# Both FFN layers of a macaron block in steps of two blocks or row tiles, on one core

## What is computed

```python
x = x + 0.5 * ffn(layernorm(x), Wr, bias, Wg, Wu, Wd, sWg, sWu, sWd)
x = x + attention(layernorm(x), ...)        # 16 heads of width 16, causal, with a decay
x = x + 0.5 * ffn(layernorm(x), ...)        # the same weights once more

def ffn(x):                                 # 1024 rows, 16 experts, hidden width 128
    probs = softmax(x @ Wr.T + bias)
    w, idx = top_k(probs, 2);  w = w / (sum(w) + 1e-9)
    y[t, e] = (silu(x[t] @ Wg[e]) * (x[t] @ Wu[e])) @ Wd[e]
    routed[t] = sum over the two chosen e of w * y[t, e]
    return routed + silu(x @ sWg) * (x @ sWu) @ sWd      # one shared expert for all rows
```

## Time and profile before

| | |
|---|---|
| median of 3 ordinary runs | 350.92 us (347.88 to 352.57) |
| profiled execution, from first to last instruction | 375.8 us |
| TensorE, matmul | 276.6 us busy, 74% |
| VectorE | 244.9 us, 65% |
| ScalarE | 167.1 us, 44% |
| GpSimd | 130.5 us, 35% |
| mean granted TensorE clock | 0.878 of full |

### The profile page before, as it was taken

One profiled execution on the slowest core, in us unless ns is written; L12 is line 12 of the kernel. 1 busy time (PEld: TensorE's weight loads), 2 busy tenths in 40 slices (PEclk: granted clock), 3 DMA queues, 4 the chain that ended last, 5 costly groups with the idle time before them and its releaser, 6 DMA issues.

```text
span 375.8 us, 6430 instructions
## 1 busy us (share of the span) xinstructions
PE 276.6 (74%) x1911; PEld 199.4 (53%) x1911; DVE 244.9 (65%) x800; ACT 167.1 (44%) x433; POOL 130.5 (35%) x181
## 2 busy tenths in 40 slices
PE   1747649888882587989999999987384598898710
PEld 1537428877771254555444444654273287787700
DVE  8686865757666871658888885466841266667616
ACT  3566604434443155357666666662321044444300
POOL 7027841555456003300445200000077125555630
PEclk9966757999997799898999999999696599999965
DMA  7996654434400617980534400000022603344127
GB/s 249 385 388 191 261 161 161 120 99 130 131 19 15 210 42 185 197 250 26 113 88 85 86 3 1 2 3 0 0 101 98 195 15 110 108 138 131 31 81 254
DMA packets 29861, 45.69 MB, mean 122 GB/s; under 512 B 5323, under 2 KB 22961, under 8 KB 29444
## 3 DMA queue, kind: packets, MB, share of 16 engines
q1 hardware_dynamic: 24164, 33.41, 29.2%
q0 software_dynamic: 5664, 11.87, 10.9%
HBM read 27.98 MB, written 20.61 MB: 129 GB/s over the span
## 4 chain that ended last, share of the span: by engine, by line
PE 54%; DVE 19%; issue 7%; DMA 7%; ACT 7%; POOL 2%; another core or an unknown queue 2%; SPq 1%; POOLq 0%; DVEq 0%; ACTq 0%
PE bank L313 23%; PE bank L1015 5%; PE bank L1054 5%; PE bank L1028 4%; PE bank L320 4%; PE bank L947 4%; PE bank L871 3%; DVE wl L1212 3%; DMA yg<-results 2%; DVE res L1384 2%; PE bank L1032 2%; DMA stk_q<-parts_d 1%; DVE xn L1227 1%; PE bank L856 1%
## 5 line engine op out<-in xcount | busy, mean ns | idle before, releaser
L568 POOL DMA_INDIRECT results<-ysb,xp x62 | 61.5, 993 | 75.4 <-DVE ysb L1351 55.6
L1440 DVE CUSTOM_DVE_ANT_0 bank<-bank,dec 128x512 f32<-128x512 f32 (+3 forms) x128 | 59.8, 518 | 18.2 <-PE bank L1015 18.0
L1312 DVE TENSOR_TENSOR hm<-sg,bank 128x128 f32<-128x128 f32 x78 | 22.3, 286 | 51.4 <-ACT sg L654 30.7
L820 ACT ACTIVATE ct<-bank 128x512 f32<-128x512 f32 (+1 forms) x96 | 45.0, 520 | 22.0 <-PE bank L1032 21.9
L654 ACT ACTIVATE sg<-bank 128x128 f32<-128x128 f32 x78 | 21.5, 276 | 63.8 <-PE bank L313 54.4
L557 POOL DMA_INDIRECT slots_x<-xn,slot x32 | 34.1, 1064 | 33.3 <-DVE slot L1289 24.3
L313 PE MATMUL bank<-wh,xT_h 128*128 x124 | 41.3, 333 | 3.7 <-DVE xT_l L1339 2.9
L700 ACT ACTIVATE xT_h<-bank 128x256 fp32r<-128x256 f32 x62 | 23.8, 386 | 34.7 <-PE bank L947 30.6
L871 PE MATMUL bank<-ident,hm 128*128 128x128 f32 x78 | 23.7, 304 | 20.4 <-issue 11.3
L1015 PE MATMUL bank<-stk_q,stk_k 96*128 96x512 bf16 (+3 forms) x128 | 34.9, 310 | 2.1 <-DMA stk_q<-parts_d 1.8
L313 PE MATMUL bank<-wh,hT_h 128*128 (+1 forms) x78 | 30.7, 394 | 7.2 <-issue 2.7
(11 more groups left out here) (186 smaller groups left out, 681.5 us busy)
## 6 DMA issues: line engine op xcount, KB each, us to landing
xp<-slots_x SPq DMA_DIRECT2D x30, 257.0 KB
w_raw<-in_experts SPq DMA_DIRECT2D x17, 384.0 KB, 8.4
yg<-results SPq DMA_DIRECT2D x16, 256.0 KB, 4.8
slots_x<-zeros SPq DMA_DIRECT2D x2, 1285.0 KB, 11.8
parts_d<-part SPq DMA_DIRECT2D x6, 384.0 KB, 3.2
stk_k<-parts_d SPq DMA_DIRECT2D x8, 192.0 KB, 3.8
stk_q<-parts_d POOLq DMA_DIRECT2D x8, 192.0 KB, 4.9
slots_x<-zeros SPq DMA_DIRECT2D x1, 1413.5 KB, 7.8
```

What stands on the lines that cost most here:

```text
L568: pool.indirect_dma_start(results, where, ysb[c % RING][:], None, bounds_check=4 * N - 1, oob_is_err=False).then_inc(s_ys[c % RING], 16)
L820: act.activation(ct[n % 6][:, a:b], bank[2 + i][:, 0:b - a], ACT.Exp).then_inc(s_exp, 1)
L1440: dve.tensor_tensor_reduce(s_i, s_i, dec[:, SEQ - w:SEQ], 1.0, NEG, ALU.add, ALU.max, mmax[g % 2][:, n % G * QT + i:n % G * QT + i + 1])\
```

## The change

Every step of the two FFN loops takes two blocks (or two row tiles) in place of one:

- The shared expert's loop has 4 steps, the block loop has NQ = 16 steps (the last one holds a single block) plus 3 for the pipeline. The order within a step stays the same: transposes of pair q, gate and up of q - 1, hidden transposes of q - 2, down products of q - 3.
- A stage's result of a pair fills one bank: 512 words for `xT`, gate and up, and down, 256 for the hidden transpose. The matmuls are the same in number and size.
- ScalarE and VectorE take both blocks in one instruction: `xT` high and low and `ysb` are 512 wide, Silu, `hm`, `hT` high and low 256, the addition to `res` 512.
- The semaphores count pairs. GpSimd waits once a pair and then issues two scatters, one for each block.
- XRING goes from 12 to 16 blocks (8 pairs loaded ahead), RING from 4 to 6. The registers with the expert addresses are still loaded four at a time.
- In the first layer the splits of weights are spread differently over the steps: two high splits on ScalarE and three low splits on VectorE per pair step.
- Some buffers share memory in another way, to make room. Nothing else changes.

```diff
-    RING = 4
-    XRING = 12
+    RING = 6
+    XRING = 16
+    REGS = 4
...
-        def over_blocks(step):
-            for b in range(NB + 3):
-                step(b, [0 <= b - k < NB for k in range(4)])
+        def blocks_in(q):
+            return min(2, NB - 2 * q)
+        def halves(tile, n):
+            return tile[:, 0:n * D].rearrange("p (i k t) -> p i k t", i=n, k=2)
+        def over_pairs(step):
+            for q in range(NQ + 3):
+                step(q, [0 <= q - k < NQ for k in range(4)])
...                                                             SyncE
-                    last = 2 * (q - QRING) + 1
-                    sp.wait_ge(s_xt, f * NB + last + 1)
-                    for b in (last - 1, last):
+                    old = q - QRING
+                    sp.wait_ge(s_xt, f * NQ + old + 1)
+                    for b in (2 * old, 2 * old + 1):
                         sp.wait_ge(*scattered(f, b))
                     load(q)
...                                                             GpSimd
                         pool.wait_ge(*landed(f, c))
-                        pool.wait_ge(s_ye, f * NB + c + 1)
-                        where = bass.IndirectOffsetOnAxis(ap=xb[c % XRING][:, D:XW].bitcast(U32), axis=0)
-                        pool.indirect_dma_start(results, where, ysb[c % RING][:], None, ...)
+                        pool.wait_ge(s_ye, f * NQ + c + 1)
+                        for i in range(blocks_in(c)):
+                            b = 2 * c + i
+                            where = bass.IndirectOffsetOnAxis(ap=xb[b % XRING][:, D:XW].bitcast(U32), axis=0)
+                            pool.indirect_dma_start(results, where, ysb[c % (RING // 2)][:, i, :], None, ...)
...                                                             ScalarE
-                act.activation(sg[par][:], bank[2 + par][:, 0:F], ACT.Silu).then_inc(s_sg, 1)
+                act.activation(sg[j % 2][:, 0:n, :], halves(bank[2 + j % 2], n)[:, :, 0, :], ACT.Silu).then_inc(s_sg, 1)
-                for i in range(NT + 2):
+                for i in range(NP_ + 1):
...
-                    if f == 0 and EARLY + i <= E:
-                        split_high(EARLY + i)
+                    if f == 0:
+                        for q in (EARLY + 2 * i, EARLY + 2 * i + 1):
+                            if q <= E:
+                                split_high(q)
...                                                             TensorE
-                three(pe, bank[2 + par][:, 0:GU], xs, ws, None).then_inc(s_gu, 1)
+                for i in range(n):
+                    mm = three(pe, bank[2 + j % 2][:, i * GU:(i + 1) * GU], xs(i), ws(i), None)
+                mm.then_inc(s_gu, 1)
-                pe.transpose(bank[4 + par][:, 0:P], hm[par][:], ident[:]).then_inc(s_ht, 1)
+                for i in range(n):
+                    mm = pe.transpose(bank[4 + j % 2][:, i * P:(i + 1) * P], hm[j % 2][:, i, :], ident[:])
+                mm.then_inc(s_ht, 1)
-                        for k in range(KT):
-                            mm = pe.transpose(bank[b % 2][:, k * P:(k + 1) * P],
-                                              xb[b % XRING][:, k * P:(k + 1) * P], ident[:])
+                        for i in range(blocks_in(q)):
+                            for k in range(KT):
+                                mm = pe.transpose(bank[q % 2][:, (i * KT + k) * P:(i * KT + k + 1) * P],
+                                                  xp[q % QRING][:, i, k * P:(k + 1) * P], ident[:])
...                                                             VectorE
-                dve.tensor_tensor(hm[par][:], sg[par][:], bank[2 + par][:, F:GU], ALU.mult).then_inc(s_hm, 1)
+                dve.tensor_tensor(hm[j % 2][:, 0:n, :], sg[j % 2][:, 0:n, :], halves(bank[2 + j % 2], n)[:, :, 1, :],
+                                  ALU.mult).then_inc(s_hm, 1)
...
-                        for q in (i + 1,) if i < 6 else (2 * i - 5, 2 * i - 4):
+                        for q in range(3 * i + 1, min(3 * i + 4, E + 1)):
                             split_low(q)
...
-                        dve.tensor_copy(ysb[r][:], bank[6 + (j - 3) % 2][:, 0:D]).then_inc(s_ye, 1)
+                        dve.tensor_copy(ysb[c % (RING // 2)][:, 0:n, :],
+                                        bank[6 + (j - 3) % 2][:, 0:n * D].rearrange("p (i d) -> p i d", i=n))\
+                            .then_inc(s_ye, 1)
```

More of the change, by code:

```diff
@@ L141, in macaron_kernel @@
         r0.close()
[L142 to L155, removed]
+        xp = [sb(f"xp{i}", [P, 2, XW], F32, r2) for i in range(4)]
+        xT = [[sb(f"xT{j}_{i}", [P, 2, KT, P], F32R, r2) for i in "hl"] for j in range(2)]
+        hT = [[sb(f"hT{j}_{i}", [P, 2, P], F32R, r2) for i in "hl"] for j in range(2)]
+        r0 = ExitStack()
+        lgT = sb("lgT", [E, N], F32, r0)
+        r0.close()
+        sg = [sb(f"sg{i}", [P, 2, F], F32, r2) for i in range(2)]
+        hm = [sb(f"hm{i}", [P, 2, F], F32, r2) for i in range(2)]
+        r0 = ExitStack()
+        lg = sb("lg", [P, NT, E], F32, r0)
+        pr = sb("pr", [P, NT, E], F32, r0)
+        tmp = sb("tmp", [P, NT, E], F32, r0)
+        oh = sb("oh", [P, 2, NT, E], F32, r0)
+        ohs = sb("ohs", [P, NT, E], BF16, r0)
+        big = sb("big", [P, NB * E], F32, r0)
+        r0.close()
+        ysb = [sb(f"ysb{i}", [P, 2, D], F32, r2) for i in range(RING // 2)]
+        iota_i = sb("iota_i", [P, NB + 1], I32, r2)
         mx = sb("mx", [P, NT], F32, r2)
@@ L197, in macaron_kernel @@
         r5.close()
-        xp += [sb(f"xp{i}", [P, 2, XW]) for i in range(2, QRING)]
+        xp += [sb(f"xp{i}", [P, 2, XW]) for i in range(4, QRING)]
         xb = [xp[i // 2][:, i % 2, :] for i in range(XRING)]
@@ L913, in w_s @@
                     return (wh, wl)[b][:, E, k * GU:(k + 1) * GU]
-                for i in range(NT + 2):
+                for i in range(NP_ + 2):
                     j = f * NJ + i
-                    if i < NT:
-                        gate_up(j, j % 2, f == 0 and i < 2, rows(i), w_s)
-                    if 0 <= i - 1 < NT:
-                        hidden_turn(j - 1, (j - 1) % 2, f == 0 and i - 1 < 2)
-                    if 0 <= i - 2 < NT:
+                    if i < NP_:
+                        gate_up(j, lambda h: rows(2 * i + h), lambda h: w_s)
+                    if 0 <= i - 1 < NP_:
+                        hidden_turn(j - 1)
+                    if 0 <= i - 2 < NP_:
                         if i - 2 >= 2:
-                            pe.wait_ge(s_ysh, f * NT + i - 3)
-                        down(j - 2, j % 2, lambda b: (wh, wl)[b][:, E, KT * GU:WE])
-                pe.wait_ge(s_ysh, (f + 1) * NT)
+                            pe.wait_ge(s_ysh, f * NP_ + i - 3)
+                        down(j - 2, lambda h, b: (wh, wl)[b][:, E, KT * GU:WE])
+                pe.wait_ge(s_ysh, (f + 1) * NP_)
                 if f == 0:
@@ L933, in ffn, with step @@
                 keep_busy(bank[5], 6)
-                def step(b, live):
-                    j, n = f * NJ + NT + b, f * NB + b
-                    if b % RING == 0 and b < NB:
-                        regs = [pe.alloc_register(f"expert{f}_{i}") for i in range(b, min(b + RING, NB))]
+                def step(q, live):
+                    j = f * NJ + NP_ + q
+                    b = 2 * q
+                    if b % REGS == 0 and b < NB:
+                        regs = [pe.alloc_register(f"expert{f}_{i}") for i in range(b, min(b + REGS, NB))]
                         pe.load(regs, bexi[0:1, b:b + len(regs)])
@@ L1328, in ffn @@
                         dve.wait_ge(s_y, j - 2)
[L1329 to L1330 removed]
+                        own = res[:, 2 * r:2 * r + 2, :]
+                        dve.scalar_tensor_tensor(out=own, in0=bank[6 + (j - 3) % 2][:].rearrange("p (i d) -> p i d", i=2),
+                                                 scalar=0.5, in1=own, op0=ALU.mult, op1=ALU.add).then_inc(s_ysh, 1)
@@ L1355, in ffn @@
+                over_pairs(step)
+                dve.wait_ge(s_ysh, NP_ * (f + 1))
                 if f == 0:
```

147 lines of the change are left out of this document (77 added, 70 removed).

## The result

The changed kernel took 356.2 us (median of 4 runs) against 351.8 us of the kernel before on the same chip (4 runs): ratio 1.020, interval 1.012 to 1.028; one of the four, at 459.1 us with a mean granted clock of 0.559, is in a slow state and is kept out of the ratio. A repeat with more runs gave 356.1 us and 1.022 (1.016 to 1.028). The change makes the kernel about 2% slower; the forecast was 356.3 us and 1.5%.

The account below looks back on a forecast made before the run. TensorE was taken to bound the loops, at 1.40 us a block. From 350.9 us, +6.0 for the drain of both layers and -0.6 for the shared expert gave 356.3 us, 1.5% slower; range 338 to 361.

Parts of the forecast that it names:

- Late completions not in ordinary runs: Block loops and second shared expert: TensorE completions 1.4 and 8 us late belong mostly to the recorded execution.
- (a): Block loops and second shared stage: late completions cost ordinary runs too, so pairs give 331 to 335 us; chance 0.16.
- (b): Same places: late completions are partly there in ordinary runs, 5 to 15 us, giving 341 to 351 us; chance 0.13.
- the sum of 26 against 24.9: Late completions priced at 22 us in both loops plus some 4 in the second layer; recorded execution 24.9 us over median.
- Wider instructions, zero: ScalarE and VectorE in the loops: 0.5 and 0.6 us saved a pair, counted zero behind busy TensorE.
- Drain, +3.0 a layer: End of each block loop: five scatters queue on GpSimd, last one 3.0 us later a layer, fill included.
- Rival (d): Block loops: VectorE paces them after all, so its saved time counts, giving 338 us; chance 0.03.
- Rival (c): GpSimd paces the loop; first scatter 4.5 us later, carried whole to the end, 4.8 a layer: 360.5 us; chance 0.15.
- Shared expert, -0.6: First layer: VectorE's weight splits end sooner, gain between 0 and 1.7 us, 0.6 taken; second layer zero.
- Rings, zero: Loads and result buffers: eight pairs loaded ahead and ysb for six blocks cost zero.

Follow-up runs that it names:

- e1_before_again: The kernel before, unchanged, recorded once more: 350.0 us, ratio 0.994 (0.988 to 1.000).
- e3_singles: The changed kernel with its rings, buffers and code, but one block or row tile per step in both FFN loops: 351.9 us, ratio 1.008 of the kernel before.
- e4_tail: The changed kernel with the block loop's last five blocks going one by one: 354.6 us, ratio 1.017 of the kernel before.
- e7_narrow: The changed kernel with each wide ScalarE and VectorE instruction issued as two narrow ones: 355.9 us, ratio 1.020 of the kernel before.
- e9_pairs_plain: The changed kernel with result scatters replaced by plain stores to fixed rows, placement left out: 345.4 us, ratio 0.989 of the kernel before.
- e10_singles_plain: The one-block kernel of e3_singles with result scatters replaced by plain stores, placement left out: 353.3 us, ratio 1.010 of the kernel before.
- e11_headtail: The changed kernel with block loops of four single blocks, eleven pairs, five single blocks: 356.4 us, ratio 1.022 of the kernel before.
- e12_shared_pairs: The changed kernel with block loops in single blocks, only the shared expert in pairs: 352.0 us, ratio 1.007 of the kernel before.
- e13_shallow: The changed kernel with a pipeline of three steps instead of four in its block loops: 354.4 us, ratio 1.016 of the kernel before.
- e8_busy_before: The kernel before with more matmuls that only keep TensorE busy, ahead of both block loops and after the first: 348.9 us, ratio 0.9985.

## Why the prediction was right, and where it was not

The stages of both loops in each trace, as us from the first transposes (first layer / second layer), read from the engines' instructions in order of time:

```
                    first scatter   last tile ready   last scatter or store starts
e1_before_again      6.7 /  8.8      47.4 / 49.3       49.2 / 51.0
e3_singles           8.6 /  6.9      49.3 / 48.2       51.0 / 49.8
after               10.5 / 10.9      46.5 / 46.8       51.6 / 52.0
e4_tail             10.7 / 10.9      47.2 / 47.3       51.6 / 51.5
e7_narrow           11.3 / 11.3      47.2 / 47.2       53.0 / 52.4
e9_pairs_plain      10.6 / 10.6      47.5 / 46.6       48.1 / 47.9
e10_singles_plain    8.4 /  8.0      49.7 / 50.8       50.2 / 51.3
e11_headtail         8.2 /  6.9      48.8 / 47.2       53.2 / 51.5
e12_shared_pairs     8.4 /  8.3      49.3 / 49.6       51.1 / 51.2
e13_shallow          9.0 /  9.5      49.4 / 50.0       51.8 / 51.9
```

**Late completions not in ordinary runs:** right. Against rivals (a) and (b): the repeat of the kernel before, without them, has a span of 348.3 us. My reason for it, that recording makes them, does not hold for recordings as such; the sum of 26 against 24.9 could only say that this one execution had them. The Trainium skill, "NOTIFIC — the notification-queue block", Interfaces, says that back pressure on the producers of trace records can stall an engine. Three of the four recordings of the kernels before and after show no sign of it: they span 348.3, 353.1 and 353.5 us, no more than the ordinary times. No run shows whether it was at work in the fourth.

**Wider instructions, zero:** right within e7_narrow's interval, and to 0.4 us a layer in the traces: its second loop takes 52.4 us instead of 52.0 (its first, 53.0, starts at the lower clock until about 58 us). The durations came as forecast. All copies of results in the kernel after (duration ns least/median/most, forms):

```profile
L1386 DVE COPY ysb<-bank x32: 425/680/692, 64.9 to 332.6; 128x512 f32<-128x512 f32 x30, 128x256 f32<-128x256 f32 x2
```

Two blocks take 680 ns instead of 2 x 418, and that is worth nothing behind a TensorE that is busy 36.00 of 36.00 us. The table of the Trainium skill, "VectorE: DVE Perf Modes", TRN2 errata, gives a VectorE copy out of PSUM a fixed part of 120 cycles at 0.96 GHz; an estimate from it, at one element a cycle, is 392 ns for width 256 and 658 for 512, and these rows agree within 7%. Rival (d) fell.

**Drain, +3.0 a layer:** the term that carried the forecast, right in place and sign, off in its make-up. Loops that run at full clock from their first gate-and-up on take 49.2 and 49.8 us from the first transposes to the last scatter in single blocks (first of e1_before_again, second of e3_singles), 51.6 and 52.0 in pairs: +2.3 a layer. The step itself was mis-sized twice, in opposite directions. From the last gate-and-up I had 7.82 us, with GpSimd free for block 26 at 2.7 us; it was 8.74, with block 26 at 3.58. The copy of 26 and 27 ended as forecast (1.70 us after the gate-and-up, 1.84 forecast), but my sum left out blocks 24 and 25, whose copy ends only 0.16 us after it, so that seven scatters and not five stand behind it. And the pair loop's last gate-and-up comes some 1.8 us earlier than the single one's (42.8 and 43.2 us after the first transposes against 44.4 and 45.2), where I had 0.5. For single blocks 4.3 was forecast and 4.7 measured (328.33 to 333.01).

**Rival (c):** its mechanism is half of the truth. The first scatter is 3.8 to 4 us later than in a single loop at full clock (10.5 to 10.9 against 6.7 to 6.9), and e4_tail shows that narrowing the tail alone doesn't take the end away. But the lateness isn't carried whole: each pair's first scatter starts when its tiles come, up to block 24, GpSimd has 0.2 us a pair to spare, and the pair loop reaches its last tile 1 to 2.5 us sooner. In the end 2.3, not the 4.8 a layer of rival (c).

**Shared expert, -0.6:** too much. The warm-up matmuls (those of `keep_busy`) start at 53.13 in the kernel after, at 53.71 in e1_before_again, released by other things:

```profile
53.13 2.72 PE L874 MATMUL bank<-below_b,ident_b 128*128 128x512 bf16 x6 [6.09 <-DMA slots_x<-xn,slot]
```

```profile
53.71 2.72 PE L856 MATMUL bank<-below_b,ident_b 128*128 128x512 bf16 x6 [4.97 <-DVE wl L1212]
```

The split of the weights ends 4 us sooner, and the scatters of the slots then hold the loop: its transposes start at 55.94 instead of 56.22. That is 0.3 us, and e12_shared_pairs shows nothing of it.

**Rings, zero:** right within 1.9 us (e3_singles against e1_before_again), and even that has another reading, next.

**What I had not seen: the attention part's clock.** The sum lacks a term. The traces of e1_before_again and of the kernel after span 348.3 and 353.1 us. Of these 4.8 us, the first loop has 2.4 and the second 1.0 (that of e1_before_again starts at the lower clock; against the second of e3_singles it would be 2.2), 2.1 lie in the attention part, where the changed code does the same work, and 0.7 come back ahead of the first loop and behind the last scatter. Windows of the start of that stretch, e1_before_again and then after:

```profile
108.00:124.00 16.00, 9.21 (x35) 4.70 (x36) 12.28 (x38) 2.63 (x7) 1.53 (x1) 0.80 0.42 132
```

```profile
108.00:124.00 16.00, 8.85 (x24) 3.75 (x25) 10.26 (x30) 1.67 (x4) 2.41 (x2) 0.50 0.42 131
```

TensorE is idle for the first rows of yg, 7.3 us in e1_before_again and 10.8 in the kernel after, and falls to 1.2 GHz (0.50). In the kernel before it was back at 2.4 GHz from about 114 us, in the kernel after from about 124. From the last scatter of the first layer to the first slot scatter of the second are 151.4 us in e1_before_again and 153.5 in after and e3_singles. So the 1.9 us by which e3_singles is slower than the kernel before lie mostly here too. Its runs spread over 350.8 to 353.2, those of the kernel before over 344.6 to 353.6, which fits a clock that rises early in some executions only, but no run shows that. Whether the change delays the clock is open. The longer idle time of the kernel after is not enough to explain it: in e3_singles TensorE idles only 7.0 us there, and the clock is back as late, at about 123. Nor is it in the changed code as such: in e9_pairs_plain, after 7.3 us, it was back by 112. e8_busy_before did not settle it.

That 356.3 was met so closely is partly luck. The base of 350.9 was 0.9 us above the 350.0 of ten runs, and 6.0 for the loops was 1.4 above the 4.6 of loops at full clock; the missing 2 and the 0.3 us that the shared expert gave less than forecast made up for both. As a ratio 1.015 was forecast and 1.022 (1.016 to 1.028) measured, so the loss itself was somewhat larger than forecast.

## What to carry to other kernels

Wider steps save instructions on engines that wait anyway, and delay the first result of each step. Before widening, look for the in-order engine behind the pipeline and divide its time per item by the loop's (here 1.29 by 1.40): near one, a late start is made up only in part (2.3 of some 4 us were left at the end), and changing the tail alone, or head and tail together, returned next to nothing here. In the pair kernel a cheaper instruction on that engine paid (0.54 for 0.98 us took off 10.7 us, with the placement left out); in the one-block kernel the same exchange gained nothing. And repeat the recording before you explain a trace that is 7% longer than the times.

## What the runs showed of the hardware

An indirect DMA to rows costs GpSimd 0.98 us and the next starts 1.29 us after it; a plain store of the same tile costs 0.54 us, two take 1.07. Behind a VectorE copy the scatter starts 0.84 us after the copy's end when GpSimd is free. A single recorded execution can be 7% longer than its kernel's times, with hand-overs from TensorE that come 1.4 to 8 us late, while the thirteen other recordings of this kernel and its variants span no more than their times. The granted clock that extra matmuls had won back by 274 us in e8_busy_before was lost again at 284, in a half-idle stretch behind them.
